# A mixture-of-experts block on one core: smaller batches of tiles late in the expert stage, two layer norms moved to GpSimd, filler matmuls, a bias in TensorE for ten tiles

## What is computed

```python
x = _layernorm(x + attn(x, w_qkv, proj, w_out, b_out))       # stage 1
expert_id = argmax(x @ wr + br, axis=-1)                     # one of E = 8
h = gelu(x @ w1[e] + b1[e])                                  # 128 -> 512
y = h @ w2[e] + b2[e]                                        # 512 -> 128
x = _layernorm(x + y)                                        # only the picked e counts
```

## Time and profile before

| what | value |
|---|---|
| median of 3 runs | 236.87 us (236.55 to 236.95) |
| profiled execution, its own time | 237.38 us |
| profiled execution, span of the trace | 235.7 us |
| mean granted clock of TensorE | 0.942 |
| busy: PE, DVE, ACT, POOL | 83%, 71%, 60%, 54% of the span |

### The profile page before, as it was taken

The page is one execution under the profiler, slowest core; times in us unless marked ns, Lnnn a source line. Parts: engine busy times, 40 slices in busy tenths (PEclk is TensorE's granted clock), DMA queues, the critical chain, the costliest instruction groups (busy, mean ns, idle before and its releaser), DMA issues.

```text
span 235.7 us, 5871 instructions
## 1 busy us (share of the span) xinstructions
PE 196.0 (83%) x1684; PEld 155.7 (66%) x1690; DVE 166.6 (71%) x539; ACT 141.5 (60%) x374; POOL 128.0 (54%) x161
## 2 busy tenths in 40 slices
PE   7989999999898887887865499899999999999000
PEld 2668888888554445444333189789989999999000
DVE  1577686867376899999998864777777766676600
ACT  3488887878476547647743527676666676666000
POOL 8338283646400108557557443463888766868860
PEclk9999999999999999999997758999999999999855
DMA  4799999999750001011011387551877787751100
GB/s 118 218 380 413 412 409 409 411 414 379 203 150 0 0 3 37 23 34 37 23 36 44 85 247 190 191 150 38 233 232 211 225 250 206 211 167 37 36 6 0
DMA packets 28416, 40.45 MB, mean 172 GB/s; under 512 B 3497, under 2 KB 18126, under 8 KB 28384
## 3 DMA queue, kind: packets, MB, share of 16 engines
q1 hardware_dynamic: 26112, 35.80, 46.9%
q0 software_dynamic: 2272, 4.27, 5.2%
HBM read 17.95 MB, written 22.56 MB: 172 GB/s over the span
## 4 chain that ended last, share of the span: by engine, by line
PE 50%; POOL 13%; issue 13%; DVE 10%; ACT 5%; DMA 4%; SPq 1%; DVEq 0%; ACTq 0%; POOLq 0%
PE pair L298 14%; PE pair L731 12%; PE pair L744 8%; POOL out_dram L506 5%; POOL sorted_rows L487 5%; PE bank L598 5%; PE bank L744 3%; POOL rstd L468 2%; DMA x_all<-sorted_rows 2%; PE pair L724 2%; PE pair L682 1%; POOL rstd L502 1%; DMA w_slot<-in_L_ffn_w_dram 1%; DMA wqkv_sb<-in_L_attn_w_qkv_dram 1%; PE bank L578 1%
## 5 line engine op out<-in xcount | busy, mean ns | idle before, releaser
L884 ACT ACTIVATE qfeat<-pair,w_sb 128x128 f32<-128x128 f32 x156 | 44.6, 368 | 27.8 <-PE pair L731 27.1
L731 PE MATMUL pair<-xsT,w_slot 128*128 128x128 f32 x312 | 43.5, 284 | 2.3 <-DMA w_slot<-in_L_ffn_w_dram 1.5
L487 POOL DMA_INDIRECT sorted_rows<-x,dest x32 | 31.9, 996 | 18.5 <-issue 11.6
L731 PEld LDWEIGHTS pair<-xsT,w_slot 128*128 128x128 f32 x312 | 39.6, 199 | 3.3 <-issue 2.6
L298 PE MATMUL pair<-wkv_part,xT_all 128*128 128x256 f32 x192 | 33.7, 320 | 2.0 <-ACT vals L811 0.8
L298 PEld LDWEIGHTS pair<-wkv_part,xT_all 128*128 128x128 f32 x192 | 28.4, 188 | 5.3 <-issue 5.3
L298 PE MATMUL pair<-xT_all,wq_part 128*128 128x512 f32 x96 | 31.7, 456 | 0.0
L744 PE MATMUL pair<-w_sb,qfeat 128*128 x232 | 31.6, 280 | 0.0
L838 ACT ACTIVATE qexp<-pair,minus_one 128x512 f32<-128x512 f32 x32 | 20.6, 678 | 15.5 <-PE pair L298 15.5
L515 POOL TENSOR_TENSOR ksum<-kfeat 128x512 f32<-128x512 f32 x12 | 16.2, 1350 | 25.0 <-DVE kfeat L954 25.0
L506 POOL DMA_INDIRECT out_dram<-x_all x26 | 26.0, 999 | 7.1 <-issue 5.8
(11 more groups left out here) (161 smaller groups left out, 362.3 us busy)
## 6 DMA issues: line engine op xcount, KB each, us to landing
sorted_rows<-pad_rows SPq DMA_DIRECT2D x11, 1584.0 KB, 23.1
w_slot<-in_L_ffn_w_dram SPq DMA_DIRECT2D x39, 256.0 KB
x_all<-in_L_attn_x_dram SPq DMA_DIRECT2D x8, 256.0 KB, 5.3
w_sb<-in_L_ffn_w_dram SPq DMA_DIRECT2D x4, 512.0 KB, 13.9
x_all<-sorted_rows SPq DMA_DIRECT2D x26, 66.0 KB, 2.6
xs<-sorted_rows SPq DMA_DIRECT2D x13, 66.0 KB, 2.8
w_sb<-in_L_ffn_b_dram SPq DMA_DIRECT2D x1, 512.0 KB, 7.6
sorted_rows<-x,dest POOLq DMA_INDIRECT x32, 2.4
```

What stands on the lines that cost most here:

```text
L487: g_.indirect_dma_start(out=sorted_rows, out_offset=bass.IndirectOffsetOnAxis(ap=dest[:, ring, i:i + 1], axis=0), in_=x1[:, ring, i, :], i ...
L731: last = mm(h_bank[t % 2][:, k * P:(k + 1) * P], w1_slot[:, t % WB, k * P:(k + 1) * P], xsT[:, t % 2, :], start=True, stop=True)
L884: a_.activation(hT[:, t % 2, k * P:(k + 1) * P], h_bank[t % 2][:, k * P:(k + 1) * P], ACT.Gelu, bias=w2_sb[:, bass.ds(w_at[t] + (FF + D + ...
```

## The change

- The batches of the second layer norm become 5 of 4 tiles (0 to 19), 3 of 3 (20 to 28) and 5 of 2 (29 to 38). Each is normalised on VectorE one step after its last tile from tile 20 on, as `NORMALISED_IN` lists. On POOL the power of the next batch now always stands in the middle of the stores of the batch ahead of it.
- The wait for the landing of the 39 stores moves from the end of POOL to the end of SyncE.
- The layer norms of groups 6 and 7 move from ScalarE to POOL: 4 `tensor_scalar` of 128x128 each. That of group 6 stands ahead of `token_numbers(G - 1)`, that of group 7 ahead of `scatter(G - 2)`.
- For tiles 0 to 9 the bias b2 is added on PE: a product of a row of ones with the bias row opens the accumulation of `down`. VectorE's second addition stays for tiles 10 to 38.
- PE gets 12 filler products ahead of `project(G - 2)`, behind waits for the sums of group 5, and 12 more behind `ranks(G - 3)`, ahead of `turn(0)`.
- VectorE does `shift_of(G - 1)` behind tile step 0 in place of behind step 1.

```diff
@@ -100,6 +100,7 @@
         w2_parts = w2_sb[:, :].rearrange("p (e x) -> p e x", e=E)
         b1_rows = sb("b1_rows", [E * FC, P])
         minus_half = sb("minus_half", [P, GT])
+        ones_row = sb("ones_row", [1, P])
         region = sb("region", [P, E])
         region_up = sb("region_up", [P, E])
 
@@ -335,9 +336,11 @@
         NA = -((E * (P - 1) - GA * GT * P) // P)
         assert XS == NA < NT and (NT - XS) * RW <= T * D
         PARTS_AT = {2: (0, 1), 3: (2,), 4: (3,), 5: (4,)}
-        BATCHES = [range(i, i + 4) for i in range(0, 32, 4)] + [range(i, min(i + 2, NT)) for i in range(32, NT, 2)]
+        BATCHES = [range(i, i + 4) for i in range(0, 20, 4)] + [range(i, i + 3) for i in range(20, 29, 3)] + [range(i, i + 2) for i in range(29, NT, 2)]
         LAST_OF = {tiles[-1]: j for j, tiles in enumerate(BATCHES)}
-        NORMALISED_IN = {7: 0, 10: 1, 13: 2, 16: 3, 20: 4, 24: 5, 28: 6, 32: 7, 34: 8, 36: 9, 38: 10, 39: 11}
+        NORMALISED_IN = {7: 0, 10: 1, 13: 2, 16: 3, 20: 4, 23: 5, 26: 6, 29: 7, 31: 8, 33: 9, 35: 10, 37: 11, 39: 12}
+
+        BIASED_BY_DVE = range(10, NT)
 
         def row_slot(t):
 
@@ -397,6 +400,8 @@
             sp.wait_ge(res_ready, G)
             for t in range(NA, NT):
                 load_rows(t)
+
+            sp.wait_ge(stored, 16 * NT)
 
 
         @block.gpsimd
@@ -426,6 +431,7 @@
             g_.memset(minus_half[:, :], -0.5)
             g_.memset(same_tile[:, :, :], 1.0).then_inc(zeroed, 1)
             g_.memset(ones_e[:, :], 1.0)
+            g_.memset(ones_row[:, :], 1.0)
             g_.memset(tiles_end[:, :], 0.0)
             pool.wait_ge(zeroed, 6)
             g_.memset(same_tile[:, :, 0:1], 0.0)
@@ -467,6 +473,15 @@
                 reach(pool, x1_ready, g - 1)
                 g_.tensor_tensor(rstd[:, par, :], var_eps[:, par, :], minus_half[:, :], ALU.pow).then_inc(rstd_ready, 1)
 
+            def layer_norm(g):
+                par, ring = g % 2, g % XR
+                pool.wait_ge(shift_ready, g + 1)
+                pool.wait_ge(rstd_ready, g + 1)
+                for i in range(GT):
+                    last = g_.tensor_scalar(x1[:, ring, i, 0:D], res[:, par, i, :], rstd[:, par, i:i + 1], shift[:, par, i:i + 1],
+                                            ALU.mult, ALU.add)
+                last.then_inc(x1_ready, 1)
+
             def token_numbers(g):
                 ring = g % XR
                 if g == 0:
@@ -525,8 +540,10 @@
             scatter(G - 3, range(0, 2))
             inverse_deviation(G - 2)
             scatter(G - 3, range(2, GT))
+            layer_norm(G - 2)
             token_numbers(G - 1)
             inverse_deviation(G - 1)
+            layer_norm(G - 1)
             scatter(G - 2, range(GT))
             scatter(G - 1, range(GT))
             inverse_deviations(0)
@@ -534,15 +551,10 @@
                 half = (len(tiles) + 1) // 2
                 for t in tiles[0:half]:
                     store(t)
-                if j + 1 < len(BATCHES) and len(tiles) == 4:
+                if j + 1 < len(BATCHES):
                     inverse_deviations(j + 1)
                 for t in tiles[half:]:
                     store(t)
-                if j + 2 < len(BATCHES) and len(tiles) < 4:
-                    inverse_deviations(j + 2)
-                if j + 2 < len(BATCHES) and len(tiles) == 4 and len(BATCHES[j + 1]) < 4:
-                    inverse_deviations(j + 2)
-            pool.wait_ge(stored, 16 * NT)
 
 
         @block.tensor
@@ -674,6 +686,11 @@
                                   start=True, stop=True, skip_group_check=True)
                 last.then_inc(attn_pre, 1)
 
+            def stay_awake(n):
+
+                for _ in range(n):
+                    mm(bank[2][:, :], ones_bf[:, :], share[:, :].to_broadcast([P, 512]), start=True, stop=True)
+
             def project(g):
                 pe.wait_ge(attnT_ready, g + 1)
                 reach(pe, res_ready, g)
@@ -739,10 +756,12 @@
                     pe.wait_ge(res_ready, G)
                     pe.wait_ge(mid_ready, G)
                 reach(pe, yx_ready, t - 3)
+                if t not in BIASED_BY_DVE:
+                    mm(y_bank[t % 4][:, 0:D], ones_row[:, :], w2_sb[0:1, bass.ds(w_at[t] + FF, D)], start=True, stop=False)
                 for k in range(FC):
                     pe.wait_ge(hT_ready, FC * t + k + 1)
                     last = mm(y_bank[t % 4][:, 0:D], hT[:, t % 2, k * P:(k + 1) * P],
-                              w2_sb[:, bass.ds(w_at[t] + k * D, D)], start=(k == 0), stop=(k == FC - 1))
+                              w2_sb[:, bass.ds(w_at[t] + k * D, D)], start=(k == 0 and t in BIASED_BY_DVE), stop=(k == FC - 1))
                 last.then_inc(y_pre, 1)
 
             def tile_step(s):
@@ -755,9 +774,13 @@
 
             for s in range(G):
                 group_step(s)
+            pe.wait_ge(res_ready, G - 2)
+            pe.wait_ge(mid_ready, G - 2)
+            keep_awake(12)
             project(G - 2)
             attend(G - 1)
             ranks(G - 3)
+            stay_awake(12)
             turn(0)
             weights_of(0)
             up(0)
@@ -897,12 +920,7 @@
             keep_rows(0)
             gelu(0)
             keep_rows(1)
-            tile_step(0)
-            layer_norm(G - 2)
-            for s in range(1, 4):
-                tile_step(s)
-            layer_norm(G - 1)
-            for s in range(4, NT):
+            for s in range(NT):
                 tile_step(s)
 
 
@@ -1154,8 +1172,9 @@
                 dve.wait_ge(y_pre, t + 1)
                 v.tensor_tensor(row, y_bank[t % 4][:, 0:D], row, ALU.add).then_inc(yx_ready, 1)
                 dve.wait_ge(yx_ready, t + 1)
-                v.tensor_tensor(row, row, w2_sb[:, bass.ds(w_at[t] + FF, D)], ALU.add).then_inc(res3_ready, 1)
-                dve.wait_ge(res3_ready, t + 1)
+                if t in BIASED_BY_DVE:
+                    v.tensor_tensor(row, row, w2_sb[:, bass.ds(w_at[t] + FF, D)], ALU.add).then_inc(res3_ready, 1)
+                    dve.wait_ge(res3_ready, t - BIASED_BY_DVE[0] + 1)
                 v.bn_stats(stats3[:, :], row).then_inc(stats3_ready, 1)
                 dve.wait_ge(stats3_ready, t + 1)
                 v.bn_aggr(mv3[:, t, :], stats3[:, :]).then_inc(mv3_ready, 1)
@@ -1171,9 +1190,9 @@
                 v.tensor_scalar(row, row, mv3[:, t, 0:1], rstd3[:, t:t + 1], ALU.subtract, ALU.mult).then_inc(y_ready, 1)
 
             def weights_of(t):
-                if t == 0:
+                if t == BIASED_BY_DVE[0]:
                     dve.wait_ge(ffn_in, 16 * (FC + 1))
-                if t < NT:
+                if t in BIASED_BY_DVE:
                     w_at[t] = offset(dve, ENG.DVE, w_tab, t, (E - 1) * WX)
 
             def tile_step(s):
@@ -1203,12 +1222,10 @@
             shift_of(G - 2)
             route(G - 2)
             residual(G - 1)
-            weights_of(0)
-            weights_of(1)
             tile_step(0)
+            shift_of(G - 1)
             rows(G - 2)
             tile_step(1)
-            shift_of(G - 1)
             route(G - 1)
             for s in range(2, NT + 1):
                 tile_step(s)
```

## The result

The changed kernel takes **234.2 us** (median of 4, 233.47 to 234.53) against 236.7 for the kernel before, measured again beside it: ratio 0.989, 95% interval [0.986, 0.992]. It is faster, by 2.5 us and not by the 8.5 forecast, and 234.2 lies above the range of 226.4 to 232.0. On another chip, with the kernel before at 236.7, it took 233.9 (ratio 0.988 [0.984, 0.993]).

A forecast was written before the change was run, and what follows sets the result against it. PE was taken to bound the kernel from 143.9 us to about 218.5, then POOL, then the closing. Terms 3.7 + 0.25 + 0.65 + 2.8 + 1.1 = 8.5 us, from 236.87 to 228.4 us; range 226.4 to 232.0.

The forecast's parts named there:

- the price of the bias product: On PE, two more f32 instructions per tile, 0.22 us by the pace of `up`; bounds 0 to 0.45.
- I take full clock: PE behind 133.4 us: with fillers the clock holds, 8.30 us of work take 4.15, step 1 starts 3.7 us earlier.
- The first dozen: 12 fillers on PE from 122.6 us, 2.75 us long, delaying nothing; `project` and `attend` end at 129.3 instead of 131.0.
- The second dozen: 12 fillers on PE from 129.5 to 132.2 us, meant to keep the clock full behind 133.4.
- the rival's case: PE's clock half again behind 133.4 us, wholly or in part: 230 to 232 us; chance 0.23.
- Waits of PE on ScalarE, and scatters: Layer norms moved to POOL at 0.5 us per operation; last scatter issued at 152.4, tile 13's rows there 2 us early.
- the hold of some 6 us: Rival: POOL held ahead of its first `tensor_scalar`, shifting scatters by 5.9 us; 232.3 us; POOL held or slow, chance 0.07.
- an operation of 1.8 us: Rival: POOL's eight `tensor_scalar` at 1.8 us each cancel the gain, at 2.1 the time is 239; chance of slower 0.03.
- The stall at tile 17: PE's late transpose at 173.41 us, waiting for rows that SyncE loaded late, disappears: -0.65 us.
- Batches and tail: Smaller batches on POOL: its last store ends 7.0 us behind PE instead of 9.8, -2.8 us.
- an earlier PE would hand the bound to POOL: End of the expert stage: if PE came still sooner, POOL's own sum would take over, with hardly more gain.
- The wait on SyncE: Closing: POOL's drain starts 0.2 us behind its last store instead of 1.3, -1.1 us; 0 if tied to landings.

The follow-up runs named there:

- a3: The changed kernel without its 24 fillers; ratio to the kernel before 0.988 [0.979, 0.996], on a chip where the latter takes some 258 us.
- c3: The changed kernel without its 24 fillers, run again; ratio to the kernel before 0.982 [0.968, 0.995], on a chip where the latter takes some 258 us.
- g2: The changed kernel with a bias product of 128 rows in place of one; 229.4 us, ratio to the kernel before 0.972 [0.967, 0.977].
- g3: The changed kernel with b2 on VectorE for all tiles, 15 fillers for the second 12, 6 more after the first transpose; 229.5 us, ratio to before 0.969.
- d4: The changed kernel with b2 on VectorE, second dozen of fillers made 15, 6 more ahead of the expert stage's first product; ratio to before 0.988 [0.977, 0.999].
- g1: The changed kernel with b2 added on VectorE for all 39 tiles; 229.3 us, ratio to the kernel before 0.969 [0.965, 0.973].
- f2: The kernel before, unaltered, run again for its trace; 236.63 us.
- c1: The changed kernel with b2 on VectorE for all tiles; ratio to before 0.986 [0.981, 0.991], on a chip where the kernel before takes some 258 us.

## Why the prediction was wrong, point by point

Two terms failed: the price of the bias product (0.22 us forecast, 0.61 measured, ten times: 3.9 us) and the step "I take full clock" behind 133.4 us (1.3 us, and 0.5 of waits beside it). The other terms came within 0.3 us.

**Fillers.** The first dozen: right in place, length (2.79 us against 2.75) and effect; the clock is full from 126.6 to 130.0 in the changed kernel, and half near there in a3 and c3 without fillers, and `project` and `attend` end at 129.4 against 129.3. The second dozen: the step "I take full clock" behind 133.4 failed in part. It was reasoned from the lengths of the idle pieces and left the piece of 1.51 us ahead of `up(0)` as the one nobody had seen held. That was the rival's case (0.23). The traces of the changed kernel show half clock there in both executions, for 3.4 and for 10.2 us; g2's trace, with the same fillers and the same piece of 1.55 us, shows none. With the piece closed the clock was full in both traces that have it (g3, d4). The term was to be -3.7; the first profile gives -1.56, so 2.1 less. From `up(0)` to step 1 it is 7.19 us there, 5.49 in g2 and 5.01 in the forecast. Of the 1.70 between the first two, 0.4 is the bias product's excess in step 0 and 1.3 the clock. The last 0.5 stands at full clock too: PE waits 0.62 and 0.18 us ahead of step 0's first product in g2 where the forecast counted 0.25 for ScalarE's copy.

**Bias product.** The term of the sum that was mis-sized, and the main cause. It was forecast at 0.22 us, with an upper bound of 0.45 for a load that is not hidden, and it measured 0.61. The step that failed was to price it by the pace of `up`, whose instructions have 128 rows each: nothing in the trace before had a 1-row load between 128-row products, and the bound thought of the product's own load, not of the load of the group behind it, which comes late as well. From step 1 to tile 13 PE took 24.9 us in place of 21.55, and 9 x 0.39 = 3.5 covers that difference of 3.4. g2 and g1 show it in the time. What makes a load of one row start late stays open.

**Waits of PE on ScalarE, and scatters.** Right. `tensor_scalar` on POOL takes 0.43 us (forecast 0.5, ends 0.29 and 1.35); neither the hold of some 6 us nor an operation of 1.8 us came. The scatters ended 1.8 us later than forecast, because they hang on `shift_of(7)`, which stands behind tile 0 on VectorE and so behind PE's late step 0; from the issue of tile 13's load (158.78) to its transpose it is 8.3 us, against 2.9 before and 4.6 forecast, and 4.5 in g2, with the product at 128 rows.

**The stall at tile 17.** As forecast: steps of 1.89 to 1.90 us from tile 13 on, without one above 1.9. The cause was read rightly: in the trace before, the rows of tile 17 were issued at 169.46 and landed 3.91 us later, where the median of these loads is 2.6. But the same stall is missing in f2, the kernel before itself. So it belongs to that one execution and not to the kernel, and counting 0.65 us for it in the median was not justified; that the sum still comes out is luck of that size.

**Batches and tail.** Right: +6.8 against +7.0 forecast and +9.7 before. The remark that an earlier PE would hand the bound to POOL is borne out by g3, with VectorE's lateness beside it.

**The wait on SyncE.** Right by the traces, 1.3 us against 1.1; not shown by a time.

With the bias product at its true price and the clock as it fell, the same sum gives 236.9 - 8.5 + 3.9 (ten products) + 1.3 (clock) + 0.5 (waits) = 234.1, against 234.2 measured. The versions without that price take 229.3 to 229.5, where the forecast had 228.4.

## What to carry to other kernels

A small product that is put between large ones is not priced by its columns alone. Count its rows too: where they differ from its neighbours', look in the trace whether the next loads still start ahead of their products, and if not, try the operand at full height, here at no further cost, since the bias stood on all partitions already. And before moving work to the engine that is the bound, compare with not moving it: left on VectorE (g1), the bias gives the same median as on PE with 128 rows (g2), because one costs PE 0.23 us a tile and the other makes VectorE late. By their medians, 229.3 to 229.5 us, g1, g2 and g3 can't be told apart; they are 3% under the kernel before and 2% under the changed one, and g3's six times lie closest together.

## What the runs showed of the hardware that was not expected

- A product with one row of weights between products of 128 rows costs 0.61 us for two instructions of 128 columns (changed kernel), against 0.23 with 128 rows (g2); the loads of it and of the group behind it start with their products and not 0.1 us ahead.
- POOL's drain at the end of a block is listed with 5.86 us behind a wait and with 8.9 to 9.2 without one. In the second case it starts ahead of the last stores' issue, and it ends 5.9 us behind the last of them in every trace, against 7.1 to 7.2 with the wait ahead of it.
- With the same instructions, the granted clock between 133 and 147 us was half for none, 3.4, 6.8 or 10.2 us in the executions looked at, of this kernel and its variants. With 12 and 12 fillers it was full in two traces of eleven (g2, c1); with the idle pieces on both sides of the first transpose at 0.2 to 0.5 us it was full in both traces that have that (g3, d4).
- On three chips the expert stage has pieces of up to 5.5 us in which three engines start next to nothing; the kernel takes 22 us longer there. Their cause is open.
